# Last three layers of a transformer block: first feed-forward pairs placed at their latest step, and the keys copied out of PSUM by ScalarE

## The chip, the cores and the metric

The kernel runs on one core of one Trainium2 chip. The metric is the device time of one execution in microseconds (us), the median of three runs. Engines are named as in the profile: PE is TensorE (PEld its weight loads), DVE is VectorE, ACT is ScalarE, POOL is GpSimd, SP is SyncE, which issues DMAs. PSUM is the memory that TensorE writes into.

## The reference, cut to what matters

```python
x = x + 0.5 * _L0_ffn_ref(_layernorm(x), ...)      # routed experts
x = x + _L0_attn_ref(_layernorm(x), ...)           # causal attention over 1024
x = x + 0.5 * _L0_ffn_ref(_layernorm(x), ...)
x = x + 0.5 * _L1_ffn_ref(_layernorm(x), w_gate, w_up, w_down)    # from here on: tail_stage
x = x + _L1_attn_ref(_layernorm(x), ...)
x = x + 0.5 * _L1_ffn_ref(_layernorm(x), w_gate, w_up, w_down)

def _L1_ffn_ref(x, w_gate, w_up, w_down):          # inner width 352
    gate, y = fp4_linear(x, w_gate), fp4_linear(x, w_up)
    return fp4_linear(silu(gate) * y, w_down)
# fp4_linear quantises both of its operands in blocks of 16: the largest magnitude / 6 is the
# scale, each value is rounded to the grid 0, 0.5, 1, 1.5, 2, 3, 4, 6 and multiplied by the scale.

def _L1_attn_ref(src, ...):                        # 16 heads of 64, four positions each
    q, k, v = split(src @ in_proj_weight.T + in_proj_bias)
    attn = softmax(q / 8 @ k.T)
    return (attn @ v) @ out_proj_weight.T + out_proj_bias
```

x is 4 x 1024 tokens of 128 values, 32 tiles of 128 tokens. Only the last three of the six layers are touched by the change.

## The kernel before

The program runs five stages one after the other: two routed feed-forwards (`moe_stage`), the first attention (`attention0_stage`) between them, and `tail_stage`, which does the last three layers in one pipeline. X, all 4096 tokens, stays in SBUF. The tail begins about 1177 us into the profiled execution.

**Pairs.** The tail's feed-forward works on pairs of token tiles, 16 pairs (p from 0 to 15) before the attention and the same 16 after it. `FIRST[p]` and `SECOND[p]` (lines 832 and 833) say at which step n the two are done; `PAIR` turns this round. Each step n is two ticks, T = 2n and T = 2n + 1; T runs over `TICKS`, and each engine writes out its work tick by tick in a loop of its own, with semaphores between the engines. So a tick has no fixed length, and the order of an engine's instructions is fixed. A pair with the step n takes four stages in four steps:

- X, step n: DVE quantises the normalised rows (`quantise`, seven instructions: five in the even tick, two in the odd one), POOL multiplies the scale back in (`scale_back`, odd tick, tile f_q).
- G, step n + 1: PE transposes (`turn_x`), ACT copies (`keep_x`), and four times in a row PE multiplies (`gate_up`, L960), ACT takes the silu (L1109), DVE forms the product (`product`, L1240), which frees the one PSUM bank for the next `gate_up`.
- H, step n + 2: the inner values are quantised by the same DVE and POOL instructions as an X of that step; a step with X and H is quantised in one go over 960 columns, X alone over 256, H alone over 704. PE turns them (`turn_h`, L969).
- D, step n + 3: the second product (`down`, L978), and DVE adds it to X (`add_back`).

ACT normalises the rows of a pair (`normalise`, tile f_src) at the end of the tick before its X, for which it needs the pair's 1/sqrt(variance).

**Attention.** It has 64 units i (8 windows of 8), one a tick, i = T - 12. PE computes queries (bank p4) and keys (bank p5) of unit i; ACT adds the bias to the queries (`keep_queries`, L1121, tile f_qb), DVE to the keys (`keep_keys`, L1252, tile f_kb). One tick later PE forms the scores, DVE picks out the block diagonal (`compact`). Eleven ticks after the queries PE turns the weights through p4 (`turn_weights`, L1020) and computes values into p5 (`values`, L935), for which p5 has to be free, so the keys must have been copied; ACT copies the values (`keep_values`, L1134). Then follow weighted sums, their copy, and the output projection (`project`, L1048). Once in eight ticks (T = 21, 29, ... 77) ACT takes the exponential, which needs another table of functions than the silu: a table load before it and one back.

**Norms.** `NORM_AT` places, for each window w, the statistics for the attention's norm at T = 9 (w = 0) or 8 + 8w; they need the first feed-forward of the pairs 2w and 2w + 1. The statistics for the second feed-forward's norm follow the projection, at every fourth tick T = 4p + 28. Both go from DVE (`remeasure`, `aggregate`) to POOL (`inverse_root`: 14 to 16 tiny instructions, each of which waits for the one before, one or two ticks later). The second norm's are in POOL's order at T = 4p + 30; for the second feed-forward of pair p.

Before, the X of the first feed-forwards stand at the steps 0 to 5 and at 6, 8, ... 24, those of the second at 17, 19, ... 47; the last tick is T = 101. The steps 17 to 25 all have an X.

Of the kernel before, what the change touches and what calls it, by code (L numbers as in the profile page):

```python
# [6 lines left out]
ALU = mybir.AluOpType  # L7
ACT = mybir.ActivationFunctionType
# [59 lines left out]
def need(engine, sem, n):  # L68

    if not isinstance(n, int) or n > 0:  # L70
        engine.wait_ge(sem, n)
# [728 lines left out]
NP2 = NT // TP2  # L800
# [5 lines left out]
CH1 = INNER1 // P  # L806
NU = CH1 * NW
# [11 lines left out]
def tail_stage(nc, C, name, Wt, out):  # L819
# [9 lines left out]

    AHEAD = 12
    FIRST = {p: p if p < 6 else 6 + 2 * (p - 6) for p in range(NP2)}
    SECOND = {p: 2 * p + 17 for p in range(NP2)}
    PAIR = {n: (p, 0) for p, n in FIRST.items()} | {n: (p, 1) for p, n in SECOND.items()}
    NTH = {n: k for k, n in enumerate(sorted(PAIR))}
    LAST = max(PAIR) + 3
# [8 lines left out]
    for T in TICKS:  # L845
        if T in NORM_AT:
            CHAINS.append((T, QT * NORM_AT[T], QT * NORM_AT[T] + QT, False))
        i = T - AHEAD
# [11 lines left out]
    with Scope(nc, name) as s:  # L860
# [9 lines left out]
        wo, bqk, bo = s.sb("wo", [P, CH1 * D]), s.sb("bqk", [P, 2 * CH1]), s.sb("bo", [P, D])  # L870
        bv, bvw = s.sb("bv", [P, CH1]), s.sb("bvw", [P, CH1, P])
        xn, xh, xl = s.sb("xn", [P, W]), s.sb("xh", [P, NT * P], F32R), s.sb("xl", [P, NT * P], F32R)
        qb, kb = ([s.sb(f"{x}{u}", [P, W]) for u in range(2)] for x in ("qb", "kb"))
# [7 lines left out]
        p4, p5, gup, tf = (s.ps(n, [P, 512]) for n in ("p4", "p5", "gup", "tf"))  # L881

        in_loaded = [s.sem(f"in_loaded{u}") for u in range(3)]
        small_loaded, high_done, wl_ready, spread, bias_made, bo_ready, biased = (
            s.sem(x) for x in ("small_loaded", "high_done", "wl_ready", "spread", "bias_made", "bo_ready", "biased"))
# [5 lines left out]
        q_ready, k_ready, v_ready, q_kept, k_kept, v_kept, s_ready, masked, reduced = (  # L891
            s.sem(x) for x in ("q_ready", "k_ready", "v_ready", "q_kept", "k_kept", "v_kept", "s_ready", "masked", "reduced"))
# [4 lines left out]
        with nc.Block() as block:  # L897
# [186 lines left out]
            def _(act):  # L1084
# [32 lines left out]
                def keep_queries(i):  # L1117
                    act.wait_ge(q_ready, i + 1)
                    need(act, s_ready, i - 1)
                    r = i % CH1  # L1120
                    a_.activation(qb[i % 2][:, :], p4[:, :], ACT.Identity, bias=bqk[:, r:r + 1]).then_inc(q_kept, 1)  # L1121

                def keep_weights(j):
                    act.wait_ge(t_ready, j + 1)
                    need(act, pv_ready, j - 1)
                    a_.activation(pt[j % 2][:, :], p4[:, :], ACT.Copy).then_inc(t_kept, 1)
# [19 lines left out]
                for T in TICKS:  # L1146
# [10 lines left out]
                    if 0 <= i < NU:  # L1157
                        if i == 0:
                            act.wait_ge(small_loaded, 64)
                        keep_queries(i)  # L1160
                    if i % CH1 == 1 and i < NU + CH1 and i > CH1:
                        w = i // CH1 - 1
                        act.wait_ge(shifted, w + 1)
                        a_.activation(Ec[:, :, :], Dc[:, :, :], ACT.Exp, scale=DH1 ** -0.5).then_inc(exp_done, 1)
# [18 lines left out]
            def _(dve):  # L1183
# [61 lines left out]
                    xs = X[:, p * TP2 * D:(p + 1) * TP2 * D]  # L1245
                    v.scalar_tensor_tensor(xs, tf[:, 0:TP2 * D], 0.5, xs, ALU.mult, ALU.add).then_inc(x_updated, 1)

                def keep_keys(i):
                    dve.wait_ge(k_ready, i + 1)
                    need(dve, s_ready, i - 1)  # L1250
                    r = i % CH1
                    v.tensor_scalar(kb[i % 2][:, :], p5[:, :], bqk[:, CH1 + r:CH1 + r + 1], None, ALU.add).then_inc(k_kept, 1)  # L1252

                def compact(j):

                    r = j % CH1
# [45 lines left out]
                for T in TICKS:  # L1302
# [6 lines left out]
                        aggregate(1)  # L1309
                    if T == 4:  # L1310
                        dve.wait_ge(bias_made, 1)
                        v.tensor_tensor(bo[:, :], bo[:, :], p5[:, 0:D], ALU.add).then_inc(bo_ready, 1)
                    if 0 <= i < NU:
                        if i == 0:
                            dve.wait_ge(small_loaded, 64)
                        keep_keys(i)
                    if n - 1 in PAIR:
                        product(n - 1, T % 2, 0)
                    quantise(n, 3 if even else 6)
# [802 lines left out]
```

## Time and profile before

| | us |
|---|---|
| median of 3 runs | 1892.03 |
| lowest, highest | 1891.06, 1893.39 |
| the profiled execution | 1895.74 |
| its span, first to last instruction | 1893.7 |
| granted TensorE clock, mean | 0.921 |

| engine | busy us | share |
|---|---|---|
| PE | 1583.6 | 84% |
| DVE | 1250.6 | 66% |
| ACT | 1020.1 | 54% |
| POOL | 707.3 | 37% |

These are averages over five stages with different limits. The change is in the tail alone, some 713 us of the span. There it has to be read step by step: which engine a step ends on. A tile named f_... in a row belongs to the tail.

### The profile page before, as it was taken

The numbers are of one execution on the slowest core, as the hardware profiler recorded it, in microseconds if no ns is written. First come the engines' busy times: TensorE is split into PE (matmuls) and PEld (weight loads), VectorE is DVE, ScalarE is ACT, GpSimd is POOL, SyncE is SP. The second block draws the span as 40 slices with busy tenths as digits, with TensorE's granted clock in tenths as the row PEclk, the third lists the DMA queues.
The fourth block names the chain that finished last, engine by engine and source line by source line (L and its number), as shares of the span: only waits on it lengthen the run. The fifth ranks groups of instructions, "written<-read, shape, count | busy, mean of one in ns | idle before, by whom it ended". The sixth has DMA issues, their size and how long they took to land. (4 is left out here: it accounts for less than half of the span.)

```text
span 1893.7 us, 35220 instructions
## 1 busy us (share of the span) xinstructions
PE 1583.6 (84%) x12162; PEld 1091.9 (58%) x12167; DVE 1250.6 (66%) x2566; ACT 1020.1 (54%) x2035; POOL 707.3 (37%) x1144
## 2 busy tenths in 40 slices
PE   6999947999999999998899993576888898878654
PEld 5668835555555555554666782354666676666443
DVE  6635558888888788882753665686668777675333
ACT  2434423788888888885333441233556656655421
POOL 0787634011111111111088763432344554443530
PEclk9999978999999999999699996688899999999876
DMA  6123421111111111110512343000000000000000
GB/s 246 36 78 85 133 69 31 34 29 34 29 29 40 29 34 29 29 29 8 201 47 84 95 119 108 3 1 1 2 2 2 8 5 7 5 7 8 4 7 8
DMA packets 50494, 83.08 MB, mean 44 GB/s; under 512 B 11124, under 2 KB 35124, under 8 KB 49652
## 3 DMA queue, kind: packets, MB, share of 16 engines
q1 hardware_dynamic: 41236, 62.07, 11.4%
q0 software_dynamic: 9088, 18.76, 2.9%
q8 instruction: 104, 1.70, 0.4%
q14 instruction: 66, 0.54, 0.1%
HBM read 43.18 MB, written 31.22 MB: 39 GB/s over the span
## 5 line engine op out<-in xcount | busy, mean ns | idle before, releaser
L1883 DVE TENSOR_REDUCE z_parts<-z_pM 128x4 f32<-128x512 f32 x576 | 373.2, 685 | 95.3 <-PE z_pM L1621 91.4
L1798 ACT ACTIVATE z_Pr<-z_pE 128x512 f32<-128x512 f32 x576 | 322.5, 597 | 84.9 <-PE z_pE L1645 82.1
L1990 POOL TENSOR_SCALAR_AFFINE_SELECT z_Pr<-z_Pr 128x512 f32<-128x512 f32 x128 | 81.6, 637 | 480.6 <-ACT z_Pr L1798 480.6
L1645 PE MATMUL z_pE<-z_QM,z_QK 128*128 128x512 f32 x576 | 250.5, 437 | 8.0 <-DMA z_QM<-z_Q 5.5
L1621 PE MATMUL z_pM<-z_KM,z_Q 128*128 128x512 f32 x576 | 233.5, 410 | 1.5 <-DVE z_Q L1873 0.9
L1645 PEld LDWEIGHTS z_pE<-z_QM,z_QK 128*128 128x128 f32 x576 | 107.6, 188 | 158.9 <-ACT z_Pr L1798 91.4
L356 POOL DMA_INDIRECT slot_results<-m_yq,m_xq x156 | 152.4, 977 | 74.8 <-ACT m_yq L561 43.1
L332 POOL DMA_INDIRECT slot_rows<-m_XN,m_dest x128 | 130.0, 1016 | 94.8 <-DVE m_dest L650 59.4
L1658 PE MATMUL z_pO<-z_Pr,z_V 128*9 128x512 f32 (+3 forms) x1536 | 159.3, 488 | 0.1
L960 PE MATMUL f_gup<-s_wguT,f_xT 128*128 128x352 f32 x256 | 117.5, 545 | 41.8 <-DVE f_src L1240 31.6
L1109 ACT ACTIVATE f_sg<-f_gup 128x176 f32<-128x176 f32 x128 | 40.7, 318 | 162.2 <-PE f_gup L960 162.0
L1134 ACT ACTIVATE f_vb<-f_p 64x256 f32<-64x256 f32 x256 | 97.0, 379 | 53.2 <-PE f_p L935 50.4
L1621 PEld LDWEIGHTS z_pM<-z_KM,z_Q 128*128 128x128 f32 x576 | 109.4, 191 | 18.3 <-DVE z_parts L1883 3.0
L1240 DVE TENSOR_TENSOR f_src<-f_sg,f_gup 128x176 f32<-128x176 f32 x128 | 42.9, 335 | 110.1 <-ACT f_sg L1109 109.8
L705 DVE TENSOR_TENSOR m_h<-m_sg,m_gu 128x512 f32<-128x512 f32 x78 | 53.7, 689 | 90.5 <-ACT m_sg L553 90.5
L553 ACT ACTIVATE m_sg<-m_gu 128x512 f32<-128x512 f32 x78 | 46.6, 598 | 101.1 <-PE m_gu L450 101.1
L1375 POOL TENSOR_SCALAR f_neg<-f_sc 128x60 f32<-128x60 f32 (+2 forms) x35 | 12.5, 356 | 214.8 <-DVE f_sc L1219 202.1
L952 PE MATMUL f_tf<-k_ident,f_q 128*128 128x128 f32 x64 | 16.7, 350 | 89.3 <-POOL f_q L1383 89.3
L960 PEld LDWEIGHTS f_gup<-s_wguT,f_xT 128*128 128x128 f32 x256 | 46.8, 216 | 65.7 <-issue 44.7
L597 DVE TENSOR_TENSOR m_h<-m_sg,m_gu 128x512 f32<-128x512 f32 x64 | 44.0, 687 | 60.9 <-PE m_gu L374 54.3
L529 ACT ACTIVATE m_sg<-m_gu 128x512 f32<-128x512 f32 x64 | 38.1, 599 | 78.5 <-PE m_gu L370 76.6
L450 PE MATMUL m_gu<-s_wh,m_xqh 128*128 x156 | 70.9, 455 | 8.4 <-issue 6.0
(274 smaller groups left out, 3888.9 us busy)
## 6 DMA issues: line engine op xcount, KB each, us to landing
slot_rows<-in_c_pad SPq DMA_DIRECT2D x2, 5070.0 KB, 24.4
m_xq<-slot_rows SPq DMA_DIRECT2D x38, 260.0 KB, 3.5
z_QM<-z_Q SPq DMA_DIRECT2D x128, 64.0 KB, 2.0
z_KM<-z_QK SPq DMA_DIRECT2D x60, 128.0 KB, 2.4
m_raw<-in_gu SPq DMA_DIRECT2D x2, 2048.0 KB, 8.7
m_XN<-slot_results SPq DMA_DIRECT2D x8, 512.0 KB, 4.2
m_raw<-slot_results SPq DMA_DIRECT2D x8, 512.0 KB, 5.9
slot_results<-m_yq,m_xq POOLq DMA_INDIRECT x156
```

What stands on the lines that cost most here:

```text
L332: g_.indirect_dma_start(xs_dram, bass.IndirectOffsetOnAxis(dest[:, k, t:t + 1], 0), XN[:, t, 2 - XO[k]:2 - XO[k] + ROW], None).then_inc(se ...
L356: g_.indirect_dma_start(y_dram, bass.IndirectOffsetOnAxis(xq[q % RING][:, j % QT, TAG[list_of(j)]:TAG[list_of(j)] + 1].bitcast(I32), 0), y ...
L450: last = mm(gu[r % 2][:, u, :], xv[q % 2][:, c], wt[:, bass.ds(es[u] * GU, GU)], start=a, stop=b)
L705: v.tensor_tensor(h[r % 2][:, :].rearrange("p (u c) -> p u c", u=2), sg[r % 2][:, :].rearrange("p (u c) -> p u c", u=2), gu[r % 2][:, :, H ...
L960: mm(gup[:, 0:INNER], xT[:, j * P:(j + 1) * P], wguT[:, c, :, :].rearrange("p a k -> p (a k)"), start=True, stop=True).then_inc(gated, 1)
L1134: last = a_.activation(vb[j % 2][a * 64:(a + 1) * 64, g * 256:(g + 1) * 256].rearrange("p (k d) -> p k d", k=4), heads, ACT.Copy)
L1621: last = mm(pM[n % 3][:, :].rearrange("p (h k) -> p h k", h=4), Q[G % 2][:, qt * P:(qt + 1) * P], KM[G % 2][:, :, kb * P:(kb + 1) * P], st ...
L1645: mm(pE[e % 2][:, :].rearrange("p (h c) -> p h c", h=4), QK[G % RING][:, kt * P:(kt + 1) * P], QM[half][:, :, q * P:(q + 1) * P], start=Tr ...
L1658: last = mm(pO[32 * h:32 * h + DH0 + 1, lo:512], V[:, (G // 4) * KT + kt, 4 * (G % 4) + h, :], Pr[j % 4][:, h, lo:512], start=(kt == 0), s ...
L1798: a.activation(Pr[j % 4][:, :, q * P:(q + 1) * P], pE[e % 2][:, :].rearrange("p (h c) -> p h c", h=4), ACT.Exp, scale=DH0 ** -0.5).then_in ...
L1883: v.tensor_reduce(parts[:, qt, kb, :], pM[n % 3][:, :].rearrange("p (h k) -> p h k", h=4), AX.X, ALU.max).then_inc(maxed, 1)
L1990: g_.affine_select(blk, blk, [[0, 4], [1, P]], ALU.is_ge, 0.0, base=0, channel_multiplier=-1).then_inc(selected, 1)
```

## The change

It alters the table of steps and one copy.

The first feed-forward of pair p moves to step 2p - 2 (for p from 2 on; pairs 0 and 1 stay), which is the last step from which its result is there when the norm of its window is measured. The X of the first ones then stand at 0, 1, 2, 4, 6, ... 28. The second ones stay at 17, 19, ... 29 for the pairs 0 to 6 and move one step down for 7 to 15, to 30, 32, ... 46. All steps from 16 to 30 have an X now, and from 30 on the X are at even steps, where they were at odd ones. The last tick is T = 99, not 101. Nothing is computed more or less often.

The keys are copied by ACT right behind the queries of the same unit, as an ACTIVATE with a bias like that of the queries; the DVE instruction goes, and its 64 waits with it. The DVE's one wait for the small constants moves to T = 4.

```diff
-    FIRST = {p: p if p < 6 else 6 + 2 * (p - 6) for p in range(NP2)}
-    SECOND = {p: 2 * p + 17 for p in range(NP2)}
+    FIRST = {p: max(p, 2 * p - 2) for p in range(NP2)}
+    SECOND = {p: 2 * p + (17 if 2 * p + 16 <= FIRST[NP2 - 1] else 16) for p in range(NP2)}
...
+                def keep_keys(i):
+                    act.wait_ge(k_ready, i + 1)
+                    need(act, s_ready, i - 1)
+                    r = i % CH1
+                    a_.activation(kb[i % 2][:, :], p5[:, :], ACT.Identity, bias=bqk[:, CH1 + r:CH1 + r + 1]).then_inc(k_kept, 1)
...
                         keep_queries(i)
+                        keep_keys(i)
...
-                def keep_keys(i):
-                    dve.wait_ge(k_ready, i + 1)
-                    need(dve, s_ready, i - 1)
-                    r = i % CH1
-                    v.tensor_scalar(kb[i % 2][:, :], p5[:, :], bqk[:, CH1 + r:CH1 + r + 1], None, ALU.add).then_inc(k_kept, 1)
...
                         dve.wait_ge(bias_made, 1)
+                        dve.wait_ge(small_loaded, 64)
...
-                    if 0 <= i < NU:
-                        if i == 0:
-                            dve.wait_ge(small_loaded, 64)
-                        keep_keys(i)
```

ACT at tick 45, where an exponential falls into a step that also has silus (f_qb and f_kb are queries and keys, f_Ec the exponential, f_sg the silu, f_pt the turned weights). Before:

```order
L1121 ACTIVATE f_qb<-f_p,f_bqk 128x512
L1164 ACT_TABLE_LOAD
L1164 ACTIVATE f_Ec<-f_Dc 128x256
L1109 ACT_TABLE_LOAD
L1109 ACTIVATE f_sg<-f_gup 128x176
L1126 ACTIVATE f_pt<-f_p 128x512
```

and now:

```order
L1121 ACTIVATE f_qb<-f_p,f_bqk 128x512
L1127 ACTIVATE f_kb<-f_p,f_bqk 128x512
L1171 ACT_TABLE_LOAD
L1171 ACTIVATE f_Ec<-f_Dc 128x256
L1109 ACT_TABLE_LOAD
L1109 ACTIVATE f_sg<-f_gup 128x176
L1132 ACTIVATE f_pt<-f_p 128x512
```

The copy of the keys has come in between the queries and everything that ACT does later in the tick.

DVE from the statistics of tick 44 into tick 45 (f_y is what `quantise` works on, f_src with f_gup the product, k_X with f_tf the added result). Before:

```order
L1194 TENSOR_SCALAR f_root<-f_var 128x2
L1229 SCALAR_TENSOR_TENSOR f_y<-f_m,f_y 128x960
L1252 TENSOR_SCALAR f_kb<-f_p,f_bqk 128x512
L1240 TENSOR_TENSOR f_src<-f_sg,f_gup 128x176
L1231 SCALAR_TENSOR_TENSOR f_y<-f_m,f_y 128x960
L1246 SCALAR_TENSOR_TENSOR k_X<-f_tf,k_X 128x256
```

and now:

```order
L1201 TENSOR_SCALAR f_root<-f_var 128x2
L1236 SCALAR_TENSOR_TENSOR f_y<-f_m,f_y 128x960
L1247 TENSOR_TENSOR f_src<-f_sg,f_gup 128x176
L1238 SCALAR_TENSOR_TENSOR f_y<-f_m,f_y 128x960
L1253 SCALAR_TENSOR_TENSOR k_X<-f_tf,k_X 128x256
```

The product follows the quantiser's step directly; the keys stood between them.

POOL at the end, around the last chain of `inverse_root` (its first instruction writes f_var, its last f_shift; f_neg is the negated scale of a step, f_q the two halves of `scale_back`). Before:

```order
L1375 TENSOR_SCALAR f_neg<-f_sc 128x60
L1358 TENSOR_SCALAR f_var<-f_var 128x2
...
L1369 TENSOR_SCALAR f_shift<-f_sq 128x2
L1383 TENSOR_TENSOR f_q<-f_y,f_neg 128x256
L1386 TENSOR_TENSOR f_q<-f_y,f_neg 128x704
```

and now:

```order
L1373 TENSOR_SCALAR f_neg<-f_sc 128x60
L1381 TENSOR_TENSOR f_q<-f_y,f_neg 128x256
L1384 TENSOR_TENSOR f_q<-f_y,f_neg 128x704
L1356 TENSOR_SCALAR f_var<-f_var 128x2
...
L1367 TENSOR_SCALAR f_shift<-f_sq 128x2
```

The chain stood between a step's scale and its `scale_back`; now it stands behind `scale_back`. It is so for all second pairs from p = 7 on.

## Rows read from the trace of the kernel before

**Rows 1.** stretches of the tail: start:end, length, busy us (instructions) of each engine, PEclk, DMA.

```profile
1326.20:1388.60 62.40, 52.71 (x725) 40.95 (x724) 38.94 (x77) 36.57 (x79) 22.12 (x45) 0.89 0.01 2
1388.60:1453.20 64.60, 54.08 (x752) 41.98 (x752) 49.52 (x103) 39.40 (x89) 31.14 (x66) 0.95 0.01 2
1453.20:1521.10 67.90, 60.36 (x796) 46.25 (x796) 53.32 (x109) 42.48 (x97) 33.40 (x67) 0.97 0.02 6
1521.10:1587.10 66.00, 57.49 (x787) 45.28 (x788) 51.55 (x105) 40.18 (x89) 33.16 (x67) 0.97 0.02 6
1587.10:1648.10 61.00, 49.48 (x741) 38.71 (x740) 40.63 (x85) 36.42 (x79) 27.68 (x62) 1.00 0.02 6
1648.10:1824.40 176.30, 131.75 (x1780) 101.74 (x1779) 90.42 (x183) 94.70 (x212) 76.13 (x151) 0.91 0.02 6
1824.40:1889.60 65.20, 32.01 (x113) 21.78 (x111) 23.71 (x44) 9.72 (x25) 12.71 (x24) 0.61 0.02 6
```

**Rows 2.** the DVE line that copies keys: its durations (ns), and who waited for it.

```profile
L1252 DVE TENSOR_SCALAR f_kb<-f_p,f_bqk x64: 650/745/753, 1253.5 to 1730.7; 128x512 f32<-128x512 f32 x64
...
  PE f_p L935: 16.6, 9
```

**Rows 3.** PE in order of time: start, us, instruction, [idle before <-releaser]; two waits of values.

```profile
1368.17 0.77 PE L935 MATMUL f_p<-f_wh,f_xh 128*128 128x512 f32 x1 [2.85 <-DVE f_kb L1252]
...
1399.66 0.77 PE L935 MATMUL f_p<-f_wh,f_xh 128*128 128x512 f32 x1 [3.66 <-DVE f_kb L1252]
```

**Rows 4.** DVE in order of time, step 14: statistics of two tiles, quantiser, keys.

```profile
1365.14 0.48 DVE L83 BATCH_NORM_STATS2 k_stats<-k_X 128x6 f32<-128x128 f32 x2
...
1366.21 1.15 DVE L1229 SCALAR_TENSOR_TENSOR f_y<-f_m,f_y 128x960 f32<-128x960 f32 x1
1367.28 0.75 DVE L1252 TENSOR_SCALAR f_kb<-f_p,f_bqk 128x512 f32<-128x512 f32 x1
```

**Rows 5.** ACT in order of time: queries and the two silus of tick 46, rows of tick 47.

```profile
1505.76 0.69 ACT L1121 ACTIVATE f_qb<-f_p,f_bqk 128x512 f32<-128x512 f32 x1
1506.82 0.32 ACT L1109 ACTIVATE f_sg<-f_gup 128x176 f32<-128x176 f32 x1 [0.37 <-PE f_gup L960]
...
1509.78 0.32 ACT L1109 ACTIVATE f_sg<-f_gup 128x176 f32<-128x176 f32 x1 [1.93 <-PE f_gup L960]
...
1520.17 0.87 ACT L1096 ACTIVATE f_src<-k_X,f_shift,f_rstd 128x128 f32<-128x128 f32 x2
```

**Rows 6.** PE in order of time: gate_up in tick 45, turn_h in tick 46.

```profile
1501.10 0.83 PE L960 MATMUL f_gup<-s_wguT,f_xT 128*128 128x352 f32 x2 [1.71 <-DVE f_src L1240]
...
1510.22 0.52 PE L969 MATMUL f_tf<-k_ident,f_q 128*128 128x128 f32 x3 [0.48 <-DVE k_X L1287]
```

**Rows 7.** POOL in order of time: a chain's end in tick 47; two rows of step 39.

```profile
1515.45 0.22 POOL L1369 TENSOR_SCALAR f_shift<-f_sq 128x2 f32<-128x2 f32 x1
...
1759.92 1.11 POOL L1362 TENSOR_TENSOR f_sq<-f_sq,f_var 128x2 f32<-128x2 f32 x1
...
1765.45 0.62 POOL L1383 TENSOR_TENSOR f_q<-f_y,f_neg 128x256 f32<-128x256 f32 x1
```

**Rows 8.** DVE in order of time, step 39: the quantiser's last instruction.

```profile
1759.83 1.16 DVE L1231 SCALAR_TENSOR_TENSOR f_y<-f_m,f_y 128x960 f32<-128x960 f32 x1
```

**Rows 9.** PE in order of time: turn_x behind POOL's f_q in steps 40, 46 and 48.

```profile
1766.13 0.69 PE L952 MATMUL f_tf<-k_ident,f_q 128*128 128x128 f32 x2 [6.88 <-POOL f_q L1383]
...
1843.89 0.69 PE L952 MATMUL f_tf<-k_ident,f_q 128*128 128x128 f32 x2 [11.22 <-POOL f_q L1383]
...
1863.87 0.69 PE L952 MATMUL f_tf<-k_ident,f_q 128*128 128x128 f32 x2 [8.18 <-POOL f_q L1383]
```

**Rows 10.** stretches, columns as in rows 1: steps 3-5, 45-50, 46-48.

```profile
1214.50:1250.70 36.20, 23.50 (x88) 15.45 (x88) 29.07 (x52) 10.49 (x29) 20.31 (x30) 0.78 0.00 0
1833.80:1889.60 55.80, 24.49 (x74) 16.00 (x74) 20.65 (x32) 7.02 (x18) 12.71 (x24) 0.57 0.01 5
1847.00:1876.70 29.70, 17.59 (x52) 11.57 (x52) 9.56 (x18) 5.33 (x14) 2.33 (x3) 0.58 0.03 9
```

## Prediction

> **What bounds the kernel now.** I first cut the tail into stretches of whole steps (the first VectorE instruction of each step, counted off along its fixed order) and read busy times by stretch [rows 1]. In the steps 20 to 23, which all carry a pair in every stage, four steps take 67.9 us and PE is busy 60.4 of them; in 28 to 31, with a new pair at every second step, 61.0 and 49.5. No engine is full: DVE has 53.3 and 40.6, ACT 42.5 and 36.4. So a step is a relay, and what counts is who is waited for.
>
> Then the time order of PE with its idle times, which names that. Three waits return. (a) In a step that has an X and no G, PE cannot start `values`, because DVE, deep in the quantiser, has not yet taken the keys out of p5: 2.85 and 3.66 us in steps 14 and 16 [rows 3], 16.6 us in nine waits over the tail [rows 2]. (b) In a full step PE waits for DVE at `turn_h`, 0.48 us, and at the second `gate_up` of an odd tick, 1.71 us in the tick with the exponential [rows 6]. (c) In the late steps PE waits for POOL's `scale_back`: 6.88 us before step 40, 11.22 before step 46, and 8.18 before step 48, which has no norm chain ahead of it [rows 9]. The end of the program is nearly nothing but such waits: steps 44 to the end take 65.2 us at a granted clock of 0.61 [rows 1].
>
> **The change part by part.** Times are made against the profile (span 1893.7 us, execution 1895.74) and taken off the median 1892.03; the profiled execution is 0.2% above it.
>
> *A, the start, steps 0 to 8.* Six of the X at steps 0 to 5 become four, so two pairs leave this stretch. Steps 3 to 5 took 36.2 us with an X each; the like steps without attention and with half of the pairs, 46 to 48, take 29.7 [rows 10]. Bounds 0 and -6.5, since the wait for the first norm in step 5 stays. I take -4, and -1 for steps 6 to 8, where less of a pair is under way as well. **-5.**
>
> *B, steps 12 to 16, the same pattern in both kernels.* Only the keys differ. The `values` waits fall away with DVE's copy, since ACT is idle there; but what follows, the queue of the quantiser and `scale_back`, is late too. Of 6.5 us [rows 3] I take two thirds, 4.3. In the even ticks DVE's copy stands between quantiser and product, 0.65 at least [rows 2], ahead of the add that PE waits for [rows 6]: 0.6 in three such ticks, 1.8. Bounds 0 and -10. **-6.**
>
> *C, steps 17 to 31, full steps.* Here the change adds work: X at all steps 16 to 30 instead of 17 to 25. By the stretches [rows 1] 24 to 27 go from 66.0 to 67.9 and 28 to 31 from 61.0 to 67.9, +8.8; step 31 stays without an X, -0.4. That is the three pairs that left the two ends of the tail, at some 3 us each. Against it, per period of four steps: 0.6 in each of the four even ticks [rows 2, 6], 0.65 in the odd tick where statistics and keys stand ahead of the product, and +0.7 in the tick of the exponential, where ACT is the one waited for and now copies the keys first. A copy by ACT I price by that of the queries, 0.69 [rows 5]: net -2.3 a period, 3.7 periods, -8.5. Bounds +9 (nothing of it) and -4. **0.**
>
> Elsewhere the copy on ACT hides: it starts when the queries' copy ends and the first silu of the tick waits for PE until 0.37 us after that; so the silu moves by some 0.3 us, but the product behind it waited for DVE anyway. The second silu has 1.93 us of idle ahead of it [rows 5]. If that cover were gone each unit would cost up to 0.69 (the slower case below).
>
> *D, steps 32 to 43, every second step an X, now at even numbers.* They took 176.3 us [rows 1], six X. Before, POOL ran the second norm's chain between the scale and the `scale_back` of an X step. In step 39 the quantiser was done at 1760.99 [rows 8] and f_q began at 1765.45 [rows 7]: 4.5 us. Now the chain comes behind `scale_back`, in the step that quantises nothing. What comes instead is DVE's statistics of two tiles in the X step, 1.1 us from 1365.14 to 1366.21 [rows 4]. Net -3.4, three times (steps 38 to 43): -10. In the three earlier ones the chain still costs part of that, and the waits for keys up to 3.66; I take -2 each, between 0 and -5: -6. **-16**, bounds -6 and -25.
>
> The links of such a chain take 1.11 us where DVE's quantiser runs and 0.22 where it doesn't [rows 7]. The Trainium skill (SBUF — State Buffer, Who interferes with whom) says that a VectorE instruction with two SBUF inputs shuts out a GpSimd one that reads SBUF until it is through; the trace agrees, 1.11 against 0.22. By that rule the chain would also become quicker in its new place, by another 3 us, though nobody waits there.
>
> *E, the end.* One step goes. The new steps 44 to 49 carry what 45 to 50 carried, 55.8 us [rows 10]; off that comes the chain ahead of step 45's `scale_back`, 11.22 - 8.18 = 3.0 [rows 9], and on it 1.4 for the last projection and its statistics, now in the same step. 54.2 against 65.2 [rows 1]. Bounds -8 and -13. **-11.**
>
> *The new wait.* `normalise` of a moved pair stands at tick 4p + 31 right after the chain's place at 4p + 30; it had two ticks more. In the full step 23 a chain at that distance ended at 1515.67 [rows 7] and ACT took up its rows at 1520.17 [rows 5], 4.5 us later. Cost 0 while that holds. The wait for the small constants moves to tick 4; POOL waits for the same ones at tick 2, and PE's bias product, which DVE awaits there anyway, needs them too: 0.
>
> Sum: -5 - 6 + 0 - 16 - 11 = -38, so 1892.0 - 38 = **1854**.
>
> **The rivals.**
> *The keys are worth nothing.* DVE is no full engine, and ACT's copy takes as long. Then B is 0, C is +8, D keeps only its -10: -5 + 0 + 8 - 10 - 11 = -18, **1874**; with half of it, 1864. For it: PE's 60.4 of 67.9 in full steps [rows 1]. Against it: PE's waits name f_kb [rows 2, 3]. The Trainium skill (Perfetto Trace Analysis, Optimizing Scalar/DVE Operations) advises such a move where VectorE is saturated; it is busy 53.3 of 67.9 us, so by that rule this is the outcome.
>
> *More than that.* Each relay that gets shorter also keeps PE at full clock, which is 0.91 in steps 32 to 43 [rows 1]; with D and B at their lower bounds the sum is -51, **1841**.
>
> *The chain comes late.* If chains run at 1.1 us a link, 14 links take 15 us, the 4.5 us of slack are gone and nine pairs wait, by what the late waits for POOL show some 3 us each: +27, -11 in all, **1881**. Against it: chains in steps without an X are quick.
>
> *Slower: ACT becomes the relay's bound.* If the keys' copy ends after the first silu could start and the product is then what PE waits for, all 64 units pay 0.69: +44 on -18, so +26, **1918**. It decides at the point where DVE reaches the product before ACT has made the silu; now DVE is later in full steps, and in steps without a quantiser PE has the projection to do meanwhile.
>
> *It doesn't do what it says:* excluded as far as the order goes, where the copy stands behind the queries and the chain behind `scale_back`.
>
> **How the numbers follow.** The forecast's case, 1846 to 1864: 0.52. More than that, 1838 to 1846: 0.18. Keys worth little, 1864 to 1876: 0.22. Chain late, 1876 to 1888: 0.05. Slower: 0.03. The range 1838 to 1874 holds the first two and most of the third, some 0.85. A measurement of this kernel tells about 0.2%, 4 us, from no change: faster by more than that 0.96, within it 0.01, slower 0.03.
>
> **What would show it.** In the profile after: no wait of PE for f_kb in front of `values` (now 16.6 us), and no larger one for ACT's keys; steps 12 to 16 shorter by some 6; steps 20 to 23 at about 65.6 and steps 24 to 31 at about 131 together; `turn_x` of the steps 38 to 43 waiting some 3 us less; from the start of step 44 about 54 us to the last VectorE instruction; a chain's f_shift done before its f_src starts. I am wrong if the second `gate_up` waits longer than now outside the ticks with the exponential, if full steps stay at 67.9 (then the keys are worth nothing), or if the steps 32 to 43 stay above 170.

## The result, and the profile after

| | before | after |
|---|---|---|
| median, us | 1892.71 (4 runs, 1891.06 to 1895.32) | 1871.82 (4 runs, 1868.50 to 1876.81) |
| the profiled execution | 1895.74 | 1873.36 |
| its span | 1893.7 | 1871.6 |
| granted clock, mean | 0.921 | 0.923 |

The ratio is 0.9891, with a 95% interval from 0.9864 to 0.9917: 21 us faster, where 38 were forecast. The direction is right and the time lies in the range, at its upper end, next to the rival in which the keys are worth nothing (1874).

The stretches of whole steps of the kernel after, columns as in rows 1; the steps 12 to 15, 16 to 19, 20 to 23, 24 to 27, 28 to 31, 32 to 43, 44 to the end, and 3 to 5:

```profile
1325.40:1385.30 59.90, 50.56 (x725) 39.19 (x724) 35.32 (x70) 41.49 (x88) 22.07 (x45) 0.94 0.01 2
1385.30:1449.60 64.30, 54.08 (x752) 42.19 (x752) 46.25 (x94) 43.71 (x96) 31.28 (x66) 0.95 0.01 2
1449.60:1516.20 66.60, 58.55 (x796) 45.30 (x796) 51.14 (x101) 46.34 (x106) 33.66 (x67) 1.00 0.02 6
1516.20:1584.00 67.80, 60.06 (x796) 46.34 (x796) 51.15 (x100) 46.27 (x105) 33.65 (x67) 0.97 0.02 6
1584.00:1650.90 66.90, 59.57 (x794) 46.38 (x794) 49.70 (x101) 45.85 (x103) 32.38 (x66) 0.97 0.02 6
1650.90:1814.80 163.90, 131.31 (x1799) 102.99 (x1800) 86.44 (x173) 102.39 (x226) 65.56 (x151) 0.94 0.02 7
1814.80:1867.60 52.80, 24.85 (x86) 16.59 (x84) 21.63 (x39) 7.01 (x18) 9.58 (x24) 0.61 0.02 5
1215.50:1251.10 35.60, 20.96 (x77) 13.41 (x76) 19.74 (x40) 8.25 (x21) 14.46 (x26) 0.72 0.00 0
```

Against [rows 1] the steps 32 to 43 and the end are 12.4 us each shorter, the steps 28 to 31 are 5.9 longer, and the full steps 20 to 23, for which 65.6 were forecast, take 66.6 instead of 67.9. The steps 3 to 5, with one X where there were three, take 35.6 instead of 36.2 [rows 10].

The same cut by the prediction's terms, in us from the first VectorE instruction of a step to that of a later one, with three experiments (below) on single parts beside it; they are worked out from the start times of DVE's instructions, one profile for each kernel:

| steps | before | after | forecast | measured | steps only | keys only | chain only |
|---|---|---|---|---|---|---|---|
| -1 to 8 (A) | 111.9 | 110.0 | -5 | -1.9 | 109.6 | 115.4 | 112.4 |
| 9 to 11 | 37.5 | 38.7 | 0 | +1.2 | 37.7 | 37.8 | 39.7 |
| 12 to 16 (B) | 78.4 | 72.4 | -6 | -6.0 | 78.6 | 72.5 | 78.5 |
| 17 to 31 (C) | 243.4 | 253.0 | 0 | +9.6 | 250.8 | 248.3 | 240.9 |
| 32 to 43 (D) | 176.4 | 163.9 | -16 | -12.5 | 167.5 | 176.2 | 162.5 |
| 44 to the end (E) | 65.2 | 52.9 | -11 | -12.3 | 53.3 | 65.2 | 61.3 |
| tail | 712.8 | 690.9 | -38 | -21.9 | 697.4 | 715.3 | 695.2 |

The experiments ran on other chips, on which the kernel before took 1893.7 to 1930.9 us. In every kernel that was profiled there, the difference lies in the stages ahead of the tail; so whole times are compared by their ratio to before on the same chip, and mechanisms by stretches of the tail. How far those hold: the changed kernel, profiled again on a chip where the tail began 39 us later, had every stretch of the last table from step 9 on within 0.3 us. The steps -1 to 8 took 108.1 us there against 110.0; nearly all of that lies in the steps 1 and 2.

### The profile page after: what moved, and what is told of

Its sections match the earlier page's. It is cut to its first block and busy times, and to the rows that moved or that the text cites. A ratio compares the mean times of both kernels' runs of the same rounds, so it can differ in the third digit from the quotient of the medians.

```text
span 1871.6 us, 35225 instructions
## 1 busy us (share of the span) xinstructions
PE 1578.1 (84%) x12167; PEld 1089.5 (58%) x12167; DVE 1221.7 (65%) x2502; ACT 1054.4 (56%) x2099; POOL 688.8 (37%) x1144
## 5 line engine op out<-in xcount | busy, mean ns | idle before, releaser
L1619 PEld LDWEIGHTS z_pM<-z_KM,z_Q 128*128 128x128 f32 x576 | 109.6, 191 | 18.0 <-DVE z_parts L1881 2.8
L553 ACT ACTIVATE m_sg<-m_gu 128x512 f32<-128x512 f32 x78 | 46.6, 597 | 100.4 <-PE m_gu L450 100.4
L952 PE MATMUL f_tf<-k_ident,f_q 128*128 128x128 f32 x64 | 16.8, 351 | 96.3 <-POOL f_q L1381 96.3
L1405 POOL TENSOR_TENSOR f_pm<-f_Pn,k_mask 128x512 f32<-128x512 f32 x64 | 83.1, 1311 | 2.4 <-DVE f_Pn L1282 2.4
L1373 POOL TENSOR_SCALAR f_neg<-f_sc 128x60 f32<-128x60 f32 (+2 forms) x35 | 12.4, 355 | 194.1 <-DVE f_sc L1226 179.2
L1381 POOL TENSOR_TENSOR f_q<-f_y,f_neg 128x256 f32<-128x256 f32 x32 | 19.9, 621 | 168.3 <-issue 168.3
```

Of the source, the lines that this page charges most:

```text
L1405: g_.tensor_tensor(pm[j % 2][:, :, :, :], Pn[:, h0:h0 + 8, :].unsqueeze(3).to_broadcast([P, 8, SEQ1, PER]), mask16[:, :].unsqueeze(1).unsq ...
L1619: last = mm(pM[n % 3][:, :].rearrange("p (h k) -> p h k", h=4), Q[G % 2][:, qt * P:(qt + 1) * P], KM[G % 2][:, :, kb * P:(kb + 1) * P], st ...
```

## The parts alone

**Steps only**: the kernel before with the two new lines for `FIRST` and `SECOND`, the keys still on DVE.

> The new table of steps, keys still copied by VectorE. The prediction's sum takes the keys out: B (steps 12 to 16) back by 6, C (17 to 31) up by 8, D keeping only the 10 us of the norm chain; -18 us against before, so about 1874. The rival theory, formed from the trace of the changed kernel (there full steps 21 and 23 last as long as before to 0.01 us, 16.76 and 15.05): in full steps the keys bring nothing, because PE waited only 0.25 to 0.48 us for VectorE in them; then the steps alone give what the full change gave (-21 us) less what the values waits cost (about 6 in steps 12 to 16 and 3 in 32 to 37): -12 us, with steps 17 to 31 within 3 us of the changed kernel's.

Measured: 1906.84 against 1922.42, ratio 0.991 (0.9885 to 0.9935).

**Keys only**: the change with the old two lines.

> The old table of steps, keys copied by ScalarE. By the prediction: -6 in steps 12 to 16, -2.3 in each period of four full steps (17 to 25, so about -5), a further -2 in each of the sparse steps with an X that had a wait for keys: -18 to -20 us in all. By the rival (full steps are not helped, and the tick with the exponential gets 0.6 to 0.7 longer where a silu follows it, six times): -6 in steps 12 to 16, about -3 later, +4 for the exponential: -5 us in all, and the steps 20 to 23 within 0.5 to 1.5 us of 67.9.

Measured: 1923.02, ratio 0.9997 (0.9982 to 1.0012). So with the old table the keys give nothing, and by whole times the table of steps alone gives what the change gives; the intervals overlap. The tail tells more. In both tables the keys save 6 us in the steps 12 to 16, as forecast. With the old table they lose them elsewhere, 4.8 in the steps 17 to 31; a further 3.5 up to step 8 lie for 2.0 ahead of the first copy of keys, where the kernel with the chain alone has them too. With the new one they lose 2.2 in the steps 17 to 31 and save 3.6 in the steps 32 to 43, and the tail is 6.5 us shorter than with the steps alone (690.9 against 697.4, one profile of each).

**Chain only**: the kernel before, with POOL running the second norm's chain one tick later, behind `scale_back`, at all pairs.

```diff
-                        if T == chain[0] + (0 if k < 2 else 1 + chain[3]):
+                        if T == chain[0] + (0 if k < 2 else 1 + 2 * chain[3]):
```

> The kernel before with one thing changed: POOL runs the second norm's chain one tick later, behind the scale_back of the same step instead of ahead of it. The prediction priced that order at 4.5 us in each of the late steps (39, 41, 43) and at 3.0 in step 45, and at part of it in 31, 35, 37: about -13.5 -3 -3 = -16 to -20 us, turn_x of steps 40, 42, 44 waiting 2.5 us instead of 6.9. If instead another arrival is close behind (the rows of ScalarE, the values' copies), the waits only change their name: under -5 us. Against it could go that the chain is then late for the normalise two ticks on: turn_x or f_am would wait for f_shift.

Measured: 1903.77, ratio 0.9898 (0.9873 to 0.9924). One number, with the old steps and the old keys, gives by whole times as much as the whole change; by the tail it is 17.6 of 21.9 us. `turn_x` of the last pairs, PE in order of time; first the kernel after (X of the steps 38, 40, 42, 44, 46), then the chain alone (X of the steps 39 and 41):

```profile
1747.94 0.69 PE L952 MATMUL f_tf<-k_ident,f_q 128*128 128x128 f32 x2 [5.58 <-POOL f_q L1381]
...
1774.43 0.44 PE L952 MATMUL f_tf<-k_ident,f_q 128*128 128x128 f32 x2 [4.14 <-POOL f_q L1381]
...
1799.55 0.69 PE L952 MATMUL f_tf<-k_ident,f_q 128*128 128x128 f32 x2 [4.15 <-POOL f_q L1381]
...
1822.83 0.69 PE L952 MATMUL f_tf<-k_ident,f_q 128*128 128x128 f32 x2 [6.74 <-POOL f_q L1381]
...
1842.19 0.69 PE L952 MATMUL f_tf<-k_ident,f_q 128*128 128x128 f32 x2 [8.17 <-POOL f_q L1381]
```

```profile
1784.57 0.69 PE L952 MATMUL f_tf<-k_ident,f_q 128*128 128x128 f32 x2 [3.20 <-POOL f_q L1383]
...
1810.33 0.44 PE L952 MATMUL f_tf<-k_ident,f_q 128*128 128x128 f32 x2 [3.20 <-POOL f_q L1383]
```

Before, the first and the fourth of these waits were 6.88 and 11.22 us, and the last, which never had a chain ahead of it, 8.18 [rows 9]. It is 8.17 still. With the chain alone the steps 38 to 43 fall from 86.5 to 75.8, with the new steps from 86.5 to 77.9. There the statistics of two tiles now stand in the X step, as the prediction set against it.

## Why the keys gave nothing in full steps

The prediction took 0.6 us off every even tick of a full step, because DVE's copy stood ahead of the quantiser's fourth instruction, f_y, and of the add that PE waits for. The copy is gone, and in most full steps the add comes no earlier. DVE in order of time in step 22 of the kernel after, and POOL beside it (f_neg is the negated scale, f_pm the attention weights spread out for PE to turn, two instructions a step):

```profile
1483.16 1.15 DVE L1223 TENSOR_REDUCE f_am<-f_src 128x60 f32<-128x960 f32 x1 [0.90 <-ACT f_src L1096]
...
1485.21 1.82 DVE L1232 SCALAR_TENSOR_TENSOR f_y<-f_src,f_rs 128x960 f32<-128x960 f32 x1
1486.96 0.28 DVE L1288 TENSOR_TENSOR k_X<-f_tf,k_X 128x128 f32<-128x128 f32 x1
...
1484.63 0.37 POOL L1373 TENSOR_SCALAR f_neg<-f_sc 128x60 f32<-128x60 f32 x1 [1.83 <-DVE f_sc L1226]
1484.96 2.99 POOL L1405 TENSOR_TENSOR f_pm<-f_Pn,k_mask 128x512 f32<-128x512 f32 x2
```

and the same place before:

```profile
1488.62 1.15 DVE L1216 TENSOR_REDUCE f_am<-f_src 128x60 f32<-128x960 f32 x1 [0.90 <-ACT f_src L1096]
...
1490.48 0.65 DVE L1252 TENSOR_SCALAR f_kb<-f_p,f_bqk 128x512 f32<-128x512 f32 x1
...
1491.29 1.20 DVE L1225 SCALAR_TENSOR_TENSOR f_y<-f_src,f_rs 128x960 f32<-128x960 f32 x1
1492.41 0.28 DVE L1287 TENSOR_TENSOR k_X<-f_tf,k_X 128x128 f32<-128x128 f32 x1
...
1490.42 2.99 POOL L1407 TENSOR_TENSOR f_pm<-f_Pn,k_mask 128x512 f32<-128x512 f32 x2
```

From the step's first instruction to the add it is 3.80 us after and 3.79 before. f_y took 1.20 and takes 1.82. In both kernels the add starts 1.99 to 2.00 us after POOL's first f_pm. So f_pm, which POOL starts as soon as the scale is there, holds f_y back, and before, the keys' copy out of PSUM ran in just that time. The Trainium skill (SBUF — State Buffer, Who interferes with whom) calls the port pair that VectorE and GpSimd share an exclusive lock, and says that the order of issue decides who blocks. The rows agree: one f_pm of 1.05 us from 1484.96 ends at 1486.0, and f_y, begun at 1485.21, then has its 1.15 ahead of it: 1487.2, measured 1487.0.

It is so in the steps 18, 19, 20, 22, 23, 24, 26, 27, 28 and 30, where f_y takes 1.81 to 1.82. In the steps 21, 25 and 29, in which DVE centres rows for the attention (f_xn), POOL is still busy with a chain, so f_pm comes later and f_y takes 1.15; there another arrival hides the gain. Step 21, DVE and PE, before and after (it starts at 1471.85 and at 1466.40):

```profile
1476.21 0.34 DVE L1240 TENSOR_TENSOR f_src<-f_sg,f_gup 128x176 f32<-128x176 f32 x1 [0.28 <-ACT f_sg L1109]
1476.46 1.11 DVE L1294 TENSOR_SCALAR f_xn<-k_X,f_mv,f_rstd 128x128 f32<-128x128 f32 x4
1477.63 0.66 PE L986 MATMUL f_p<-k_ident,f_xn 128*128 128x128 f32 x4 [1.04 <-DVE f_xn L1294]
```

```profile
1470.75 0.34 DVE L1247 TENSOR_TENSOR f_src<-f_sg,f_gup 128x176 f32<-128x176 f32 x1 [0.65 <-ACT f_sg L1109]
1471.01 1.11 DVE L1295 TENSOR_SCALAR f_xn<-k_X,f_mv,f_rstd 128x128 f32<-128x128 f32 x4
1472.17 0.66 PE L986 MATMUL f_p<-k_ident,f_xn 128*128 128x128 f32 x4 [1.41 <-DVE f_xn L1295]
```

DVE is ready 0.37 us earlier and waits that much longer for the silu, so f_xn, for which PE waits, starts 4.61 us into the step in both kernels, and both steps take 16.8 us.

Four kernels test the lock. In the first, on top of the change, POOL makes the f_pm of each tick before it makes f_neg, not after:

```diff
+                    if 0 <= i - L_TURN + 1 < NU:
+                        expand(i - L_TURN + 1)
                     if some and even:
                         negate(n)
...
-                    if 0 <= i - L_TURN + 1 < NU:
-                        expand(i - L_TURN + 1)
```

> The changed kernel with POOL's spreading of the weights (f_pm) put ahead of the negated scale in each even tick. In the changed kernel's trace the quantiser's fourth step (f_y from f_src) takes 1.82 us in full even ticks where it took 1.20 before, and POOL's f_pm runs for 2.99 us across it. Theory one, they get in each other's way: f_pm then runs before the quantiser's scale is there, f_y takes 1.15 to 1.2 again, turn_h's wait of 0.25 us for VectorE's add goes, and 0.2 to 0.5 us are won in each full even tick and up to 0.6 in sparse ones with an X: -5 to -8 us against the changed kernel, about 1865. Theory two, PE's own work fills full steps (16.76 and 15.05 us): f_y gets shorter, the steps don't, under 2 us in all.

Measured: 1897.79, ratio 0.9868 (0.9844 to 0.9893). f_y stayed at 1.81 to 1.82 in the even steps from 18 to 30: POOL makes the even tick's f_pm before f_neg, so the odd tick's now follows f_neg at once, and that one collides. In the steps 19, 23 and 27 a chain stands between the two; f_y fell to 1.15 there, and the steps from 15.05 to between 14.4 and 14.5. The steps 17 to 31 took 249.5 us instead of 253.0. The second makes both f_pm wait until f_y is through:

```diff
-                    if 0 <= i - L_TURN + 1 < NU:
-                        expand(i - L_TURN + 1)
+                    if even:
+                        if some and (0 <= i - L_TURN + 1 < NU or 0 <= i - L_TURN + 2 < NU):
+                            pool.wait_ge(qstep, QSTEPS * (quantised(n) - 1) + 4)
+                        for j in (i - L_TURN + 1, i - L_TURN + 2):
+                            if 0 <= j < NU:
+                                expand(j)
```

> The changed kernel, but POOL forms both f_pm of a step (turned weights spread out) in its even tick, behind DVE's fourth quantiser instruction f_y; before, the first ran from 0.3 us after f_sc on, beside f_y. Theory 'the saved time is lost on the shared port': in full steps f_y took 1.20 us with DVE's keys copy ahead of it and takes 1.81 to 1.82 us without, since POOL's two-input f_pm is now the first of the two; so the quantiser's fourth step ended 3.8 us after the step's start in both kernels. Then here f_y falls back to 1.15 to 1.20 in the median, the steps 20 and 21 fall from 16.76 to about 16.2, the steps 17 to 31 from 186.4 to about 178, and the time by 6 to 10 us, 0.5% of the changed kernel's. Theory 'full steps hang on PE and ACT': f_y gets shorter and the steps stay at 16.76 (time within 3 us of the changed kernel). A loss is possible where the chain, now behind both f_pm, ends too late for the next step's rows: steps 19, 23, 27 above 15.1.

Measured: 1908.91 against 1930.85, ratio 0.9887 (0.9871 to 0.9904). DVE and POOL in step 22:

```profile
1520.21 1.15 DVE L1232 SCALAR_TENSOR_TENSOR f_y<-f_src,f_rs 128x960 f32<-128x960 f32 x1
1521.56 0.29 DVE L1288 TENSOR_TENSOR k_X<-f_tf,k_X 128x128 f32<-128x128 f32 x1 [0.21 <-PE f_tf L1048]
...
1521.44 2.07 POOL L1405 TENSOR_TENSOR f_pm<-f_Pn,k_mask 128x512 f32<-128x512 f32 x2 [1.44 <-DVE f_y L1232]
```

f_y takes 1.15 and two f_pm 2.07 together. DVE now waits for PE at the add, not PE for DVE. The steps 20, 22 and 24 fall by some 0.36 us each and 19, 23, 27 and 31 by 0.7, but 17, 21, 25, 29 and 33 rise by 2.2 to 2.3. In those DVE centres rows in the even tick, and the second f_pm runs into that. In step 21:

```profile
1503.72 1.88 DVE L1295 TENSOR_SCALAR f_xn<-k_X,f_mv,f_rstd 128x128 f32<-128x128 f32 x4
...
1502.68 2.06 POOL L1405 TENSOR_TENSOR f_pm<-f_Pn,k_mask 128x512 f32<-128x512 f32 x2
...
1505.65 0.82 PE L986 MATMUL f_p<-k_ident,f_xn 128*128 128x128 f32 x4 [2.17 <-DVE f_xn L1295]
```

> The changed kernel with both f_pm of a step behind f_y, as in the run before, except in the steps whose even tick centres rows (17, 21, 25, ...), which keep their order. There the second f_pm had run into DVE's four f_xn (1.88 us against 1.11) and those steps had risen by 2.3 us each. Theory 'shared port in both places': steps 17, 21, 25, 29 fall back to 16.8 (17: 18 to 20), steps 20, 24, 28 stay at 16.4 and 19, 23, 27 at 14.4, so the steps 17 to 31 take about 180 and the time is 4 to 7 us below the changed kernel's. Rival 'the relay pays it back in the next step': 20 to 23 stay above 66.6.

Measured: 1905.12 against 1928.77, ratio 0.9875 (0.9855 to 0.9895), and the changed kernel itself on the same chip 1905.69, ratio 0.9879 (0.9862 to 0.9895):

> The changed kernel once more, beside the kernels of this call, so that they are compared with it on one chip. Expected: the ratio 0.989 to before that it had on the first chip, between 0.986 and 0.992. If it comes out at 0.985 or lower, the gains of the variants over it (ratios 0.984 to 0.987) are the chip's and not theirs.

The steps 17 to 31 took 246.7 us instead of 253.0 (253.3 when the changed kernel was profiled again): the mechanism is as stated, in the steps named (21, 25 and 29 at 16.8, 20, 24 and 28 at 16.4, 23 and 27 at 14.4). Step 17 alone stayed long, 19.6 against 18.0, with a granted clock of 0.91. The whole time shows next to nothing of it: in these profiles the steps up to 5 took 2.8 us more than in the changed kernel (the whole tail takes 685.1 against 688.9), the stages ahead of it wander too, and the intervals overlap. The fourth kernel asks whether this place of f_pm is a gain by itself: new steps, keys on DVE, the order of the third.

> The new table of steps with the keys still on DVE, and both f_pm behind f_y outside the steps that centre rows. It asks what the keys' copy is worth on ACT once POOL's f_pm is out of the way; the same order with keys on ACT took 246.8 us for the steps 17 to 31 and the two kernels without the new f_pm place took 250.8 (keys on DVE) and 253.0 (on ACT). Theory 'on DVE the copy only filled the time in which f_y would have waited for the port': here f_y stays near 1.2 us and steps 17 to 31 stay at 250 to 251, so with the port free the keys on ACT are worth 4 us there. Rival 'the f_pm place is a gain by itself': the steps 17 to 31 fall to about 247 here too, and the keys are worth nothing in full steps under any order. The tail: 697 by the theory, 691 to 693 by the rival.

Measured: 1876.61 against 1893.73, ratio 0.9917 (0.9903 to 0.9932). The steps 17 to 31, in us:

| | f_pm beside f_y | f_pm behind f_y |
|---|---|---|
| keys on DVE | 250.8 | 250.3 |
| keys on ACT | 253.0 | 246.7 |

Neither edit alone gains there; together they gain 4. Of the 6.3 us between the two kernels with keys on ACT, 2.9 lie in the steps 26 and 30, where the granted clock is now 1.00 instead of 0.91. Either f_y waits for the lock, or the copy stands ahead of it; taking away one of the two leaves the other. (The steps 32 to 37 rose from 89.6 to 93.4 in this kernel; why stays open.)

## The tick of the exponential

The prediction put 0.7 us on each tick of an exponential. By single steps, keys on ACT cost 2.4, 0.6, 1.9 and 1.5 us in the steps 18, 22, 26 and 30 against the steps alone. ACT and PE in step 26 of the kernel after:

```profile
1558.18 0.70 ACT L1127 ACTIVATE f_kb<-f_p,f_bqk 128x512 f32<-128x512 f32 x1
1558.90 1.28 ACT L1171 ACT_TABLE_LOAD   x1
...
1562.75 1.10 PE L960 MATMUL f_gup<-s_wguT,f_xT 128*128 128x352 f32 x2 [2.28 <-DVE f_src L1247]
1563.15 1.12 PE L935 MATMUL f_p<-f_wh,f_xh 128*128 128x512 f32 x1
...
1565.06 1.13 PE L1012 MATMUL f_pS<-f_kb,f_qb 64*64 64x64 f32 x32
```

The experiment leaves the keys with DVE in these ticks, ahead of the product:

```diff
                         keep_queries(i)
-                        keep_keys(i)
+                        if not (i % CH1 == 1 and i > CH1):
+                            keep_keys(i)
```

> The changed kernel, but in the seven ticks in which ACT takes the exponential the keys stay with DVE. Theory 'the keys lengthen the tick of the exponential': ACT is there what PE waits for (second gate_up 2.28 us, before 1.71; 3.57 against 2.94 in tick 37, followed by matmuls at half clock), so steps 18, 22, 26 and 30 fall from 18.67, 17.98, 19.26 and 18.86 to about 18.0, 17.4, 17.8 and 18.2, and the tail by 3 to 4 us. Theory 'it is the steps' new pattern': these steps stay as they are, within 0.2 each.

Measured: 1905.38 against 1930.85, ratio 0.9861 (0.9843 to 0.9879). The steps 18, 22, 26, 30 fell to 17.7, 17.4, 17.4, 17.4, but the steps 9 to 11 rose by 1.8, step 17 by 1.1 and the end from step 44 on by 1.4, and so the tail stayed at 690.5. PE in its step 26, then the whole step in the kernel after and in this one (columns as in rows 1):

```profile
1598.36 0.83 PE L960 MATMUL f_gup<-s_wguT,f_xT 128*128 128x352 f32 x2 [1.70 <-DVE f_src L1248]
1598.76 0.66 PE L935 MATMUL f_p<-f_wh,f_xh 128*128 128x512 f32 x1
```

```profile
1549.70:1569.00 19.30, 16.48 (x199) 12.61 (x200) 13.80 (x29) 14.29 (x30) 5.28 (x5) 0.91 0.03 9
```

```profile
1585.90:1603.30 17.40, 14.74 (x199) 11.38 (x200) 14.39 (x30) 13.50 (x29) 5.29 (x5) 1.00 0.03 10
```

The copy costs the relay 0.58 us (2.28 against 1.70), as priced. The other 1.3 go with the clock: the granted clock of the step is 0.91 instead of 1.00, and `values` and scores run at the lower level of 1.2 GHz, 1.12 and 1.13 us instead of 0.66 and 0.69 at 2.4. In step 22 PE waited 2.28 us as well and kept its clock: the granted clock of that step is 1.00 and it takes 18.0 us, while the steps 18 and 30 have 0.82 and 0.91. The third kernel above, with keys on ACT and waits of 2.29 us in the steps 22, 26 and 30, had 1.00 in all three, which took 17.6 us each. The steps 18, 22 and 30:

```profile
1415.90:1434.60 18.70, 14.83 (x180) 11.39 (x181) 13.53 (x28) 13.42 (x28) 5.29 (x5) 0.82 0.01 2
1483.20:1501.10 17.90, 14.68 (x199) 11.32 (x199) 13.64 (x28) 13.98 (x30) 5.29 (x5) 1.00 0.02 8
...
1617.50:1636.40 18.90, 16.03 (x199) 12.66 (x200) 13.72 (x28) 13.84 (x29) 5.28 (x5) 0.91 0.02 8
```

## The first pairs, and all together

The changed kernel with the old line for `FIRST`. The second pairs then have their X at 17, 19, ... 25, 26, 28, ... 46.

> The changed kernel with the first pairs back at their old steps (0 to 5, 6, 8, ... 24), the second ones one step earlier from p = 5 on (26, 28, ... 46), keys on ACT. Theory 'moving the first pairs only fills steps': the steps 24 to 31 fall from 134.7 to about 127, the stretch up to step 8 goes up by 2 at most, the rest stays, so 5 to 6 us less than the changed kernel. Rival 'the start pays for it', as predicted: the steps -1 to 8 rise by 5 and it comes out even.

Measured: 1901.54 against 1930.85, ratio 0.9844 (0.9830 to 0.9857). The steps 28 to 31 are back at 61.0 (after: 66.9), the steps 6 to 8 up by 2.1, the rest within 1.4 either way; the tail 688.2 against 690.9. So moving the first pairs costs 6 us in the late steps and brings 2 at the start. By whole times this kernel beats the change: its interval lies just below both of the changed kernel's (0.9864 to 0.9917 and 0.9862 to 0.9895). But they come from other chips, and the tails differ by only 0.7 to 2.7 us. PE in step 4 of the kernel after, where the changed table has an X and no G:

```profile
1236.31 0.69 PE L952 MATMUL f_tf<-k_ident,f_q 128*128 128x128 f32 x2 [5.64 <-POOL f_q L1381]
...
1237.47 1.54 PE L960 MATMUL f_gup<-s_wguT,f_xT 128*128 128x352 f32 x2 [0.47 <-ACT f_xT L1103]
```

Before, with the G of another pair in that step, PE waited 0.16 us at the same place, and its next `gate_up` took 0.86 us. Now PE waits until `scale_back` is through, and the next products run at the lower level of the clock. Step 3 is 0.5 and step 4 is 0.9 us longer than before, though each carries less of a pair, and step 5 is 1.8 shorter.

Two kernels put edits together: the old `FIRST` with both f_pm behind f_y, and then the old `FIRST` with the order of f_pm that spares the centring steps and the keys on DVE in the five ticks of an exponential from tick 37 on.

> The first pairs at their old steps, the second ones one step earlier, keys on ACT, and both f_pm behind f_y: the two edits of the runs before together. If they add: 5 to 6 plus 4 to 8 us less than the changed kernel, since there are fewer full steps for the second to act on. If both only take slack from the same relay: no better than the better one of the two.

Measured: 1907.98 against 1930.85, ratio 0.9878 (0.9859 to 0.9898), tail 691.0: the loss in the centring steps eats it, as in the other kernel with that order (the steps 21 and 25 take 19.0).

> All that helped in one kernel: first pairs at their old steps, the second ones one step earlier from p = 5 on, keys on ACT but on DVE in the five exponential ticks from tick 37 on, both f_pm behind f_y except in the steps that centre rows. If the edits add: the tail at 680 to 684 against 688.2 for the first-pairs edit alone and 690.9 for the changed kernel, ratio to before 0.980 to 0.983. If they share one relay's slack: 686 or more, ratio about 0.985.

Measured: 1902.76 against 1928.77, ratio 0.9870 (0.9852 to 0.9887); the changed kernel beside it had 0.9879. Its tail takes 684.6 us, the shortest of all, and its steps 17 to 31 241.5 against 253.3. By whole times it is 2.9 us below the changed kernel, within the intervals, so no more is claimed than that the tail is 4 us shorter in one profile. The kernel with only the old `FIRST` has the lowest ratio; it did not run beside that one on the same chip, and the two intervals overlap.

## Why the prediction was right or wrong

**A, the start: too large.** Forecast -5, measured -1.9 in this profile and -3.8 in the second one of the same kernel; the kernel before was profiled once. The -1 for steps 6 to 8 was -2.4 in both. The -4 came from the steps 3 to 5, which fell by only 0.5 to 0.8. The step that failed took 46 to 48 as the like of 3 to 5. With two X, one G and one H fewer, PE is busy 20.8 us in the steps 3 to 5 instead of 23.5, but waits 13.2 instead of 11.7, 5.64 of them in step 4, and its granted clock is 0.72 instead of 0.78.

**B, steps 12 to 16: the sum right, the working partly by luck.** Forecast -6, measured -6.0, and the kernels with one part alone give it to the keys (72.5 against 78.6). PE's waits for keys are gone, 9.5 us in these steps, and nobody waits for L1127 in the trace after. But 7.3 us of waits for POOL's f_q have come in their place. PE's last such wait in step 16, before [rows 3] 3.66 us for f_kb, and after:

```profile
1397.46 0.44 PE L952 MATMUL f_tf<-k_ident,f_q 128*128 128x128 f32 x2 [2.82 <-POOL f_q L1381]
```

The five steps as a whole, before and after:

```profile
1326.20:1404.60 78.40, 64.08 (x894) 50.02 (x894) 51.54 (x107) 43.88 (x95) 28.84 (x57) 0.87 0.01 2
```

```profile
1325.40:1397.80 72.40, 59.36 (x892) 46.20 (x892) 46.98 (x97) 49.96 (x105) 26.39 (x50) 0.95 0.01 2
```

PE's waits together fell by 1.3 us only (14.3 to 13.0). The other 4.7 are PE's busy time for the same work, at a granted clock of 0.95 instead of 0.87. The prediction had 4.3 from the waits and 1.8 from the add; the clock stood only in its rival "more than that".

**C, full steps: the step that failed.** Forecast 0, measured +9.6. The added pairs were sized well: +8.4 forecast, +7.4 with the steps alone. The -8.5 for the keys was +2.2, so the term that failed is the net 2.3 us saved in each period of four full steps. Of its parts, the 0.65 us in the odd tick with statistics was too small: the steps 20, 24 and 28 fell by 1.8, 1.7 and 1.3 against the steps alone. Step 20's second `gate_up` on PE, before and after:

```profile
1466.05 1.51 PE L960 MATMUL f_gup<-s_wguT,f_xT 128*128 128x352 f32 x2 [2.13 <-DVE f_src L1240]
```

```profile
1461.87 0.83 PE L960 MATMUL f_gup<-s_wguT,f_xT 128*128 128x352 f32 x2 [1.48 <-DVE f_src L1247]
```

The wait is shorter by 0.65, exactly the forecast, and the clock gives the rest: 0.91 in step 20 before, 1.00 after. The 0.6 us in each even tick was zero, by the port in most steps and by the silu in 21, 25 and 29. The 0.7 in the exponential's tick was 0.6 plus the clock, up to 2.4. The wrong reading was in (b). PE's wait for DVE's add, from which the 0.6 was taken, was 0.48 us in the steps 19 and 23 and 0.25 in 20, 21, 22, 24 and 25, so 0.6 was more than PE ever waited there. And those 0.48 us [rows 6] were taken as the time of DVE's copy; that DVE's next instruction had a neighbour on POOL was in the trace (f_pm at 1490.42, 2.99 us for two of 1.05), and the prediction applied the rule of the port to the chain alone.

**D: mechanism right, size somewhat too large.** For the steps 38 to 43 -10 was forecast, measured -8.8, and the chain alone gives -10.7. PE waits 7.5 us less in them (28.7 to 21.2), but the three `turn_x` waits themselves fell by 1.3, 2.7 and 0.9 us, where some 3 each were expected. For 32 to 37 it was -6 and came -3.7, nearly all of it the keys (89.6 with the steps alone). That the chain alone gains 3.2 there with X at odd steps, and the new table nothing, stays open.

**E: right.** Forecast -11, measured -12.3. One step less and the wait ahead of the last but one X 6.74 instead of 11.22; the chain alone gets 3.9 of it.

**The rivals.** The keys worth nothing was the outcome by time (ratio 0.9997 alone), but with the new table the tail says otherwise (6.5 us for the keys). And in full steps the reason was another than the rival's in the main: the time saved on DVE was POOL's lock, and ACT is the one waited for in one tick of eight; only in the steps 21, 25 and 29 did DVE simply have slack. That rival set B to 0, where the keys did give their 6. The chain coming late did not happen: the first one of a moved pair was through at 1610.0 us, and ACT took up its rows at 1616.65 (L1096). ACT as the bound of all ticks did not happen either; in the steps 17 to 31 PE's waits of 2.28 us and more, all behind a silu, stand only where a table is loaded.

## What to carry to other kernels

Before an instruction is taken off an engine, look at what the next one there will meet at its new, earlier time; a copy out of PSUM may be filling a time in which a neighbour holds the port anyway. A chain of tiny instructions in front of the one that the next engine waits for was worth more here than the copy on another engine: one number moved it behind and gave 1%. And a wait priced in idle time can cost about three times that, where the clock falls behind it (1.9 us for 0.58 in step 26, 1.8 for 0.65 in step 20).

## What the runs showed of the hardware

- A SCALAR_TENSOR_TENSOR of 128x960 on DVE takes 1.15 us alone and 1.82 when a two-input TENSOR_TENSOR of POOL (1.05 us alone) began 0.25 us ahead of it. Two such POOL instructions with it between them take 2.99 us instead of 2.07. A TENSOR_SCALAR of DVE out of PSUM (0.65 us) ran beside f_pm at full speed; four TENSOR_SCALAR of 128x128 from SBUF to SBUF took 1.88 instead of 1.11.
- After the same 2.28 us of idle time PE's next matmuls ran once at the upper level of its clock (step 22) and once at the lower (step 26, 128x512 in 1.12 us instead of 0.66). Nor does the length of the wait decide it: before, a wait of 2.94 us in step 18 left the step's granted clock at 1.00, and one of 2.13 us in step 20 came with 0.91. What tells them apart stays open.
- In the changed kernel, profiled on two chips, each stretch of the tail from step 9 on repeated within 0.3 us, while the start of the tail lay between 1174.0 and 1216.1 us over the profiled kernels.
